# Second experts of an attention and mixture-of-experts layer: finishing each tile by itself instead of in pairs, and scattering it one step earlier

## The reference, cut to what matters

```
x        = layernorm(x + attention(x))                    # 4096 tokens x 256
flat_e   = best expert of the best group, of 8            # one expert a token
combine  = g_prob * e_prob                                # its weight
h        = relu(x @ w1[flat_e] + b1[flat_e])              # 512 wide
moe_out  = combine * (h @ w2[flat_e] + b2[flat_e])
x        = layernorm(x + moe_out, ln2_g, ln2_b)
output   = x1 + x                                         # x1: what went into this block
```

## Time and profile before

| | before |
|---|---|
| median of three runs | 2404.18 us (2403.26 to 2404.22) |
| the profiled execution | 2391.44 us |
| its span | 2389.6 us |
| granted clock of TensorE, mean over the span | 0.949 |
| busy, share of the span: PE, PEld, DVE, ACT, POOL | 85%, 46%, 64%, 49%, 45% |
| last part: first transposes, first scatter, last scatter | 2190.4, 2215.3, 2385.9 us |

### The profile page before, as it was taken

How to read it: one execution, slowest core, us unless ns; L and a number is a source line. 1 busy time by engine, 2 the same in 40 slices (tenths; PEclk the granted TensorE clock), 3 DMA queues, 4 the chain that set the end, 5 groups by cost and what they waited for, 6 DMA issues and landing times.

```text
span 2389.6 us, 33476 instructions
## 1 busy us (share of the span) xinstructions
PE 2039.4 (85%) x11408; PEld 1095.2 (46%) x11408; DVE 1524.2 (64%) x3278; ACT 1161.6 (49%) x2719; POOL 1065.4 (45%) x840
## 2 busy tenths in 40 slices
PE   7999999999899999875768966989999998864996
PEld 4555555555555555542336842323333332222664
DVE  4348687677868686849834537656766666253665
ACT  5676666766666766631112430455555545530121
POOL 2017475665847484845745522102222111045675
PEclk9999999999999999987889987999999999986999
DMA  8224533434100000041234732111111150212222
GB/s 289 80 72 169 180 135 116 142 111 147 58 24 5 15 5 14 1 135 32 89 131 144 218 98 78 31 43 46 39 53 51 46 179 16 67 36 93 80 84 69
DMA packets 175729, 204.59 MB, mean 86 GB/s; under 512 B 19305, under 2 KB 157417, under 8 KB 175306
## 3 DMA queue, kind: packets, MB, share of 16 engines
q1 hardware_dynamic: 124442, 121.75, 16.0%
q0 software_dynamic: 16752, 45.84, 6.3%
q10 hardware_dynamic: 34368, 34.87, 4.3%
HBM read 83.75 MB, written 114.46 MB: 83 GB/s over the span
## 4 chain that ended last, share of the span: by engine, by line
PE 56%; DVE 15%; POOL 9%; ACT 9%; issue 6%; another core or an unknown queue 2%; DMA 2%; SPq 1%; POOLq 0%; DVEq 0%; ACTq 0%
PE ps L1887 11%; POOL prod L853 8%; ACT m_pt L2046 6%; PE ps L580 3%; PE ps L607 3%; PE ps L566 3%; DVE pb L735 3%; PE ps L591 3%; PE ps L617 3%; DVE sc L865 3%; PE ps L1901 3%; PE ps L2256 3%; PE ps L2248 2%; PE ps L1309 2%; PE ps L1845 2%
## 5 line engine op out<-in xcount | busy, mean ns | idle before, releaser
L1978 DVE TENSOR_REDUCE m_mx<-ps 128x2 f32<-128x1024 f32 x256 | 311.6, 1224 | 172.0 <-PE ps L1866 170.0
L735 DVE CUSTOM_DVE_ANT_0 pb<-ps,bias,snl 128x128 f32<-128x128 f32 (+3 forms) x512 | 260.4, 547 | 226.5 <-PE ps L580 225.2
L2046 ACT ACTIVATE m_pt<-ps 128x1024 f32<-128x1024 f32 x256 | 260.2, 1023 | 289.2 <-PE ps L1887 289.2
L853 POOL TENSOR_TENSOR prod<-qs,kvs 128x1024 f32<-128x1024 f32 x120 | 283.9, 2393 | 163.5 <-issue 142.3
L853 POOL TENSOR_TENSOR prod<-sc,kvs 128x1024 f32<-128x1024 f32 x120 | 280.4, 2369 | 98.6 <-ACT sc L971 85.8
L1887 PE MATMUL ps<-m_q,m_k 32*128 32x512 f32 x1024 | 274.1, 647 | 50.7 <-ACT m_pt L2046 39.8
L931 ACT ACTIVATE pb<-pb,mst 128x129 f32<-128x129 f32 (+3 forms) x512 | 283.5, 560 | 19.1 <-DVE mst L735 17.1
L1866 PE MATMUL ps<-m_k,m_q 32*128 32x512 f32 x1024 | 276.2, 660 | 9.0 <-DVE m_mx L1978 8.0
L580 PE MATMUL ps<-kz,qT 64*128 64x128 f32 (+3 forms) x1024 | 186.0, 442 | 0.0
L2065 POOL DMA_INDIRECT m_yg<-ye_scratch,e_pos x64 | 63.1, 987 | 270.2 <-DVE m_x L1966 232.9
L591 PE MATMUL ps<-ident,pb 128*128 128x128 f32 x1280 | 179.3, 279 | 0.5 <-DVE mst L735 0.4
(11 more groups left out here) (329 smaller groups left out, 3790.5 us busy)
## 6 DMA issues: line engine op xcount, KB each, us to landing
xh_scratch<-zt SPq DMA_DIRECT2D x43, 768.0 KB, 8.5
xe_scratch<-zt ACTq DMA_DIRECT2D x32, 1024.0 KB, 4.8
ye_scratch<-e_ys SPq DMA_DIRECT2D x36, 256.0 KB
hw_w<-in_w SPq DMA_DIRECT2D x16, 512.0 KB, 6.2
xin<-in_x SPq DMA_DIRECT2D x8, 512.0 KB
y_scratch<-e_y SPq DMA_DIRECT2D x8, 512.0 KB
m_x<-y_scratch SPq DMA_DIRECT2D x8, 512.0 KB, 4.1
x1c_scratch<-e_x SPq DMA_DIRECT2D x8, 512.0 KB
```

The source lines that it names most:

```text
L735: dv.tensor_tensor_reduce(pb.ap[:, j, SEG[t]:SEG[t] + n], rS.of(("S", b, p, t, j)).ap[:, 0:n], k.bias[:, h, CAUSAL[t]:CAUSAL[t + 1]], -1.0 ...
L853: e.tensor_tensor(out, one, two, ALU.mult).then_inc(*k.c.did(*product_done(step, b, t, u)))
L1978: dv.tensor_reduce(x.ap[:, t, 64 * half:64 * half + 64].rearrange("p (i r) -> p i r", i=2)[:, :, 16], score_ring(k, b).of((b, g, t, half)) ...
L2046: ac.activation(p.ap[:, 2 * half:2 * half + 2, :], k.qE.of((b, g, kt, half)).ap, ACT.Exp).then_inc(*did("m_exp", b, g, kt, half))
```

## The change

Four edits, all in the loop of the last part.

- VectorE adds epsilon for every tile by itself, one column wide, and finishes tile j-4 (`h_res`) in every step, between the first bias of tile j-1 and the work on tile j-3. The pairs at the end of odd steps are gone.
- GpSimd takes the power of each tile's variance by itself, in every step, one column wide.
- The scatter is that of tile j-5 instead of j-6. It stands where it stood, in front of the next fetch.
- So the loop ends one step earlier, with 44 steps instead of 45.

```diff
-    return [("h_more",)] + [("h_expert", j) for j in range(NS_H + 6)] + [("h_end",)]
+    return [("h_more",)] + [("h_expert", j) for j in range(NS_H + 5)] + [("h_end",)]
...
+            if 0 <= j - 4 < NS_H:
+                n = j - 4
+                z, l = k.hz.of(n), k.lnh[n // 2 % 3]
+                w.wait_ge(at("h_cen", n), at("h_rs", n), at(f"i_hxg{n % HG}", n))
+                dv.scalar_tensor_tensor(z.ap[:, :], z.ap[:, :], l["rs"][:, n % 2:n % 2 + 1], k.hxg.of(n).ap[:, :], ALU.mult, ALU.add).then_inc(*did("h_res", n))
             if 0 <= j - 3 < NS_H:
                 n = j - 3
...
-                if last_of_two(n):
-                    dv.tensor_scalar(l["ve"][:, 0:i + 1], l["mv"][:, 0:i + 1, 1], EPS, None, ALU.add).then_inc(*did("h_ve", n // 2))
+                dv.tensor_scalar(l["ve"][:, i:i + 1], l["mv"][:, i:i + 1, 1], EPS, None, ALU.add).then_inc(*did("h_ve", n))
                 dv.scalar_tensor_tensor(z.ap[:, :], z.ap[:, :], l["mv"][:, i, 0:1], k.g2[:, :], ALU.subtract, ALU.mult).then_inc(*did("h_cen", n))
-            for n in ended(j):
-                z, l = k.hz.of(n), k.lnh[n // 2 % 3]
-                w.wait_ge(at("h_cen", n), at("h_rs", n // 2), at(f"i_hxg{n % HG}", n))
-                dv.scalar_tensor_tensor(z.ap[:, :], z.ap[:, :], l["rs"][:, n % 2:n % 2 + 1], k.hxg.of(n).ap[:, :], ALU.mult, ALU.add).then_inc(*did("h_res", n))
...
-            if 0 <= j - 6 < NS_H:
-                n = j - 6
+            if 0 <= j - 5 < NS_H:
+                n = j - 5
...
-            if 0 <= j - 3 < NS_H and last_of_two(j - 3):
-                p, l = (j - 3) // 2, k.lnh[(j - 3) // 2 % 3]
-                c = (j - 3) % 2 + 1
-                w.wait_ge(at("h_ve", p), at("mhalf", 0))
-                po.tensor_tensor(l["rs"][:, 0:c], l["ve"][:, 0:c], k.mhalf[:, 0:c], ALU.pow).then_inc(*did("h_rs", p))
+            if 0 <= j - 3 < NS_H:
+                n = j - 3
+                i, l = n % 2, k.lnh[n // 2 % 3]
+                w.wait_ge(at("h_ve", n), at("mhalf", 0))
+                po.tensor_tensor(l["rs"][:, i:i + 1], l["ve"][:, i:i + 1], k.mhalf[:, 0:1], ALU.pow).then_inc(*did("h_rs", n))
```

## The result

| | before | changed |
|---|---|---|
| median, 11 runs each | 2400.95 us (2393.46 to 2405.66) | 2386.62 us (2381.70 to 2395.15) |
| ratio of the two | | 0.9941, 95% interval 0.9922 to 0.9959 |
| the profiled execution, its span | 2391.44, 2389.6 us | 2389.18, 2387.4 us |

What follows compares the result with a forecast made beforehand. TensorE with unchanged pauses was taken to pace the last part, and the scatter chain to set its end. The loop gains nothing and the end 5.1 us (3.33 plus 1.8): 2404.18 - 5.1 = 2399.1 us, range 2394 to 2408.

Steps and rivals of the forecast that it cites:

- What bounds the last part: Last part: TensorE sets the pace, 4.10 us a tile plus 14.3 us of pauses; behind it the scatter chain sets the end.
- the gathers' 23.5 us: GpSimd's nine gathers wait 23.5 us for VectorE's pairs; TensorE waits for none of it, so removing it gains nothing.
- VectorE: Loop: 19 more epsilon operations, 3.2 us in idle time; the new wait for GpSimd's power costs nothing.
- the cover of 4.7: Loop: VectorE may come up to 4.7 us later before it costs TensorE anything.
- GpSimd's step: Loop: single powers lengthen GpSimd's step from 4.26 to 4.54 us, bounds 4.40 and 4.85; it still keeps up with TensorE.
- The end: Scatters behind TensorE's end: one link of 3.33 us less and a head 1.8 earlier, -5.1 us, bounds 3.3 to 6.0.
- The loop gains nothing: Loop: TensorE's pitch stays 4.10 us and its pauses as before; freed gathers become work and smaller waits, no gain.
- Rival C: Loop: TensorE's pauses shrink too; a third of 14.3 us gives 2394.3 (6 in 100), all 2384.8 (2 in 100).
- rival A: Loop: GpSimd becomes the slower pace, +4.4 to +9.2 us, in the middle 2411.0; 12 in 100.
- The port rule: VectorE's epsilon operations may block GpSimd through the shared port: 3.2 us at most, 0.08 a step, gain still 5.1.
- Carrying the profile over to the median: Whole kernel: the profiled execution took 2391.44 us, the three-run median 2404.18; the difference is carried over unchanged in us.

Runs made afterwards that it cites:

- the end part alone: Kernel before with only tiles 34 to 38 (second run: 28 to 38) finished singly and scattered five steps behind: ratios 0.9996 and 1.0005.
- e_scat6: Changed kernel with its scatter six steps behind instead of five: 2357.36 us, ratio 1.0003 to the kernel before; repeats 1.0004 and 0.9996.
- the loop part alone: Kernel before with only tiles 0 to 33 finished singly and scattered five steps behind: ratio 0.9958 on the second chip, 1.0010 on the fifth.
- e_pow2: Changed kernel with each power computed twice, first into a tile nobody reads: 2391.47 us, ratio 1.0016 to the kernel before.
- e_hg6: Kernel before with six residual buffers instead of four, so no gather waits for a pair: 2353.26 us, ratio 0.9995; repeats 1.0006 and 0.9992.

## Why the prediction was wrong, point by point

- **What bounds the last part.** "TensorE with its pauses" is right for the chips of the first kind: stretch 182 to 185 us with 14 to 16 us of pauses. That the gathers' 23.5 us "aren't the prize" is neither shown nor refuted.
- **VectorE.** Right: 39 L2306 of 0.153 us. Its waits for the power are 3.3 us in five there, 1.1 the longest, and up to 1.8 on the third chip, well inside the cover of 4.7.
- **GpSimd's step.** Mis-sized, on the safe side: 4.36 us, not 4.54. The power is 0.58 where it follows work, near the low bound taken from L2078; my row, 0.687, was of a power that had just waited. The 4.26 for the old step was read from one pair of steps. On the third chip the pairs of the kernel before in which GpSimd never waits longer than its usual 0.3 us take 8.37 to 9.05 us, in the middle 8.60; this one, by its scatters, takes 8.80:

```profile
2287.08 1.27 POOL L2530 DMA_INDIRECT out_y<-h_z,h_xs  x1 [0.18 <-issue]
...
2291.41 1.01 POOL L2530 DMA_INDIRECT out_y<-h_z,h_xs  x1 [0.30 <-issue]
...
2295.88 1.05 POOL L2530 DMA_INDIRECT out_y<-h_z,h_xs  x1 [0.19 <-issue]
```

  That middle is 4.30 a step. The changed kernel's such steps take 4.36 to 4.63 us there, in the middle 4.42, and 4.36 on the first chip: the single powers cost GpSimd some 0.06 to 0.12 us a step, not the 0.28 of the prediction (4.54 - 4.26).
- **The end.** Right in mechanism and size, as far as the traces show it: forecast -5.1 with bounds 3.3 and 6.0, and 6.6 us from TensorE's end to the last scatter; measured 6.9 instead of 11.7 (-4.8) on the first chip, 8.1 instead of 12.1 (-4.0) on the third. What it gives in time by itself isn't shown clear of noise: both runs with the end part alone gained nothing, at a loss of their own making where the distance changes, and the changed kernel was 4.0 and 1.2 us faster than e_scat6.
- **The loop gains nothing.** This is the step that failed. "TensorE's pauses as before" was a constant of the sum; on the third chip they fell from 15.0 to 6.3 us and the stretch from 182.0 to 173.9, on the second chip the loop part alone took 8.6 us off. The end's 5 and the loop's 8 give 13, against 14.3 and 12.4 measured. On the first chip itself this is inferred: the one profile of the changed kernel there has 16.4 us of pauses, and its kernel before has no profile near 2401. Rival C named this outcome at 2394.3 for a third of the pauses and 2384.8 for all; the median of 2386.62 lies between, where 8 in 100 stood. Its one argument against, that the gathers' waits end after the pauses, spoke of one possible cause and not of all. The rows put part of these pauses down to nobody, and the rest to an engine that itself waits for TensorE; a stretch that nobody explains is an unknown of both signs, not a zero.
- **The pace of GpSimd** (rival A). Not there on the first chip. On the other kind of chip it is the limit, and takes back 1.9 of the 4.0 us of the way out on the fourth chip and 3.0 of 2.6 on the fifth; e_pow2 shows that it is near on the third chip too: 0.52 us more a step cost 15.7 us.
- **The port rule.** With 39 operations instead of 20 their longest is 0.155 us, where the earlier trace rows had 0.407, and the power beside them doesn't grow. The rule of the Trainium skill ("SBUF — State Buffer", "Who interferes with whom") has no price here that these rows show. What did grow is `h_res`: 0.48 us in the middle before, 0.55 in the changed kernel on the third chip, where it now often starts right behind the power. That is time of VectorE, and no run tells why.
- **Carrying the profile over to the median.** The forecast started from 2404.18, a median of three runs; that of eleven is 2400.95, so 3.2 of the 12.5 us by which it missed come from the base and not from the mechanism. And it rested on a profiled execution well below the median. That should have widened the range downwards: whatever the excess is, the change could remove it. The two profiles differ by 2.3 us and the medians by 14.3, but which part of the kernel holds the difference on the first chip isn't shown.

**What stays open.** What the pauses are. They came in the five profiles of kernels that finish by pairs on the first kind (11.0 to 15.7 us), shrank with single finishing in three (9.1, 6.3, 2.5), not in the fourth (16.4, the first chip's), vanished where GpSimd held TensorE at 4.88 us, and never came on the other kind. One reading is that they come only while TensorE keeps to its own step of 4.10 us, and that GpSimd's even step of 4.36 us in the changed kernel holds it just off that; this is argued, not shown, and the 16.4 speaks against it. A longer lead of the fetches also went with fewer pauses, in both kernels (15.5 to 11.0, 6.3 to 2.5), each in one profile. How much the pauses of one and the same kernel vary from run to run on one chip wasn't measured. Single finishing with the scatter six behind, and pairs with six residual buffers, weren't run on a chip that has pauses.

## What to carry to other kernels

Idle time of the bounding engine that the trace puts down to nobody is a term with two bounds, nothing and all of it; an edit that changes the rhythm around it can remove it without touching what it seems to wait for. Price the tail of a pipeline by its chain, links times distance: in the traces of the two chips with pauses that came out to about 1 us. And measure a small change on more than one chip: here the same edit was worth 0.55 to 0.6% on two and 0 to 0.1% on two others.

## What the runs showed of the hardware

- **Two kinds of chip.** The same kernel takes 2388 to 2401 us on three chips and 2353 to 2356 on three others; in the last part TensorE's stretch is 182 to 185 us against 167 to 169 in e_hg6 and its repeats, and the pauses, 14 to 16 us against 1.5, cover the difference. As much or more lies ahead of that part, which starts at 2188 to 2196 us on the first kind and at 2164 to 2179 on the other. Each was visited once, as far as the record tells, so chip and occasion can't be told apart.
- **TensorE's results come later than its records say.** In the kernel before on the third chip:

```profile
2268.37 1.88 PE L2248 MATMUL ps<-hw_w,h_sT 128*128 x4
2274.48 3.43 PE L2256 MATMUL ps<-hw_w,h_hT 128*128 x8 [4.22 <-issue]
```

  The transposes of L2264 that this product needs are recorded before 2268.37, yet ScalarE's relu of them starts only at 2273.75, after 7.48 us without work. VectorE, too, reads the product recorded from 2265.91 to 2267.88 only at 2271.06:

```profile
2273.75 0.60 ACT L2504 ACTIVATE h_hT<-ps 128x512 f32<-128x512 f32 x1 [7.48 <-DMA x1c_scratch<-e_x]
```

```profile
2271.06 0.42 DVE L2293 TENSOR_TENSOR h_z<-ps,hw_b 128x256 f32<-128x256 f32 x1 [2.18 <-DMA w_awq<-in_attn_wq]
```

  The DMAs in the brackets were issued before 1368 and at 40 us and had long ended, so they released nothing here. As the ends of matmuls are modelled, the likely reading is that TensorE was some 5 us behind its records; no run tests it. The product after the pause takes 3.43 us instead of 1.89; the granted clock falls to half (1.2 GHz) for 3.4 us there, behind the pause and not ahead of it (the clock stands behind the five busy times: 1.00, then 0.50):

```profile
2272.00:2274.00 2.00, 0.00 (x0) 0.00 (x0) 1.21 (x6) 0.25 (x1) 1.28 (x2) 1.00 0.35 105
2276.00:2278.00 2.00, 2.00 (x7) 1.54 (x6) 0.00 (x0) 0.00 (x0) 0.39 (x1) 0.50 0.22 70
```

- **A power of one column** takes 0.58 us on GpSimd behind other work and up to 0.74 after a wait; one of two columns 0.73. **An indirect DMA** costs GpSimd 0.95 to 1.1 us of issue and up to 1.3, with some 0.30 between two. With three of them and a one-column power no step was shorter than 4.35 us.
